# Batch normalisation, two group normalisations and two convolution stacks as one pipeline of 48 strips

## The reference

```
x = x + attention(gn(x))                        # dilated, shifted windows
x = x + relu(batch_norm(grouped_conv3x3(gn(x))))
x = x + stack(gn(x), weights 2)
x = x + stack(gn(x), weights 3)
```

## Time and profile before

| what | value |
|---|---|
| median of three runs | 2486.26 us |
| the profiled execution | 2484.12 us |
| its span, first to last instruction | 2482.3 us |
| TensorE busy | 2034.6 us, 82% |
| VectorE busy | 1684.5 us, 68% |
| ScalarE busy | 1167.8 us, 47% |
| GpSimd busy | 1079.6 us, 43% |

### The profile page before, as it was taken

The page is one execution under the profiler, slowest core; times in us unless marked ns, Lnnn a source line. Parts: engine busy times, 40 slices in busy tenths (PEclk is TensorE's granted clock), DMA queues, the critical chain, the costliest instruction groups (busy, mean ns, idle before and its releaser), DMA issues. The chain is left out here.

```text
span 2482.3 us, 75405 instructions
## 1 busy us (share of the span) xinstructions
PE 2034.6 (82%) x30446; PEld 1079.9 (44%) x30446; DVE 1684.5 (68%) x3438; ACT 1167.8 (47%) x2597; POOL 1079.6 (43%) x1227
## 2 busy tenths in 40 slices
PE   6588878887898899868994029999997499999996
PEld 5455545554555455535552003444442133333332
DVE  5588898889888988872223964666665456556553
ACT  6476666666666566632223414444442044433330
POOL 0277767776777777749502823222220131111100
PEclk8799999999999999979997559999999599999997
DMA  8300000000000000002224941444444323444444
GB/s 228 98 23 22 22 19 22 22 22 19 22 22 22 20 23 22 22 14 68 97 96 159 405 181 49 116 146 130 143 126 114 118 58 104 122 129 129 117 101 103
DMA packets 249921, 215.55 MB, mean 87 GB/s; under 512 B 132592, under 2 KB 237808, under 8 KB 247536
## 3 DMA queue, kind: packets, MB, share of 16 engines
q1 hardware_dynamic: 249584, 210.81, 28.6%
HBM read 78.29 MB, written 75.50 MB: 62 GB/s over the span
## 5 line engine op out<-in xcount | busy, mean ns | idle before, releaser
L1176 POOL TENSOR_SCALAR l_x<-l_x,l_scale,l_shift 128x384 f32<-128x384 f32 x192 | 155.6, 810 | 600.5 <-PE banks L1403 600.5
L418 POOL TENSOR_TENSOR at_prob<-at_prob,at_inv 128x512 f32<-128x512 f32 x288 | 294.1, 1042 | 116.7 <-DVE at_inv L558 111.5
L484 ACT ACTIVATE at_prob<-at_prob 128x512 f32<-128x512 f32 x288 | 181.9, 632 | 335.2 <-DVE at_prob L548 335.1
L1366 PE MATMUL banks<-l_a,l_taps 128*32 128x384 f32 x3456 | 310.9, 490 | 8.4 <-ACT l_r L1226 8.4
L1381 PE MATMUL banks<-l_above,l_taps 128*32 128x384 f32 x1728 | 307.4, 489 | 4.0 <-issue 1.8
L1381 PE MATMUL banks<-l_below,l_taps 128*32 128x384 f32 x1728 | 306.2, 489 | 0.0
L600 PE MATMUL banks<-at_xn,at_w 128*64 128x256 f32 x2336 | 287.5, 389 | 1.8 <-ACT at_xn L436 1.4
L1236 ACT ACTIVATE l_above<-l_below 96x384 f32<-96x384 f32 x144 | 75.5, 524 | 416.6 <-DVE l_below L1309 416.6
L1309 DVE SCALAR_TENSOR_TENSOR l_below<-banks,l_b,l_old 128x384 f32<-128x384 f32 x144 | 89.0, 618 | 218.7 <-PE banks L1381 188.7
L1295 DVE COPY l_old<-l_a 32x384 f32<-32x384 f32 x576 | 208.5, 362 | 26.1 <-ACT l_a L1213 14.9
L399 POOL TENSOR_TENSOR at_turn<-at_turn,at_tables 128x256 f32<-128x256 f32 x292 | 215.4, 759 | 1.7 <-ACT at_turn L455 1.7
(11 more groups left out here) (142 smaller groups left out, 3625.2 us busy)
## 6 DMA issues: line engine op xcount, KB each, us to landing
l_x<-x_mid SPq DMA_DIRECT2D x48, 768.0 KB, 4.4
l_rows<-l_r SPq DMA_DIRECT2D x768, 48.0 KB, 2.0
at_k_bd<-at_k SPq DMA_DIRECT2D x1168, 16.0 KB, 1.8
load_raw<-in_x SPq DMA_DIRECT2D x36, 512.0 KB, 5.0
y<-c_y SPq DMA_DIRECT2D x96, 192.0 KB
bn_y<-y SPq DMA_DIRECT2D x8, 2304.0 KB, 11.6
x_mid<-x_res SPq DMA_DIRECT2D x8, 2304.0 KB, 15.7
x_mid<-l_x SPq DMA_DIRECT2D x24, 768.0 KB, 3.7
```

Of the source, the lines that this page charges most:

```text
L418: nc.gpsimd.tensor_tensor(prob[i][p][:, :, :], prob[i][p][:, :, :], inv[i][p][:, :].unsqueeze(2).broadcast_to([P, HEADS, WIN]), ALU.mult). ...
L484: nc.scalar.activation(prob[j % 2][p][:, :, :], prob[j % 2][p][:, :, :], ACT.Exp).then_inc(s["exped"], 1)
L1366: last = nc.tensor.matmul(grid(acc(k)[block_rows(c), :]), e[:, dy + 1, dx, :], a[:, k % A_RING, rows_, dx:dx + SIDE], start=(dy, dx) == TA ...
```

## The change

`batch_norm_stage`, gn2, gn3 and both `stack_stage` calls go. `conv1_stage` also stores the centred image to HBM, next to `y`. One `tail_stage` does the rest:

```diff
-            conv1_stage(sh, c1_w, c1_b, y)
-            batch_norm_stage(sh, bn, y, x_mid)
+            conv1_stage(sh, c1_w, c1_b, both[:, 1, :], both[:, 0, :])
         sh.recycle()
-        group_norm_stage(sh, "gn2", TILES)
-        stack_stage(sh, "l2", w2, x_mid)
-        sh.recycle()
-        group_norm_stage(sh, "gn3", TILES)
-        stack_stage(sh, "l3", w3, x_mid, out)
+        tail_stage(sh, (w2, w3), bn, both, out)
```

In the convolution stage, on SP, for every group g:

```diff
+                sp.wait_ge(s["centred"], g + 1)
+                at = slice(g * C1_SPAN, (g + 1) * C1_SPAN)
+                sp.dma_start(x_dram[:, at], sh.x[:, at]).then_inc(s["x_stored"], 16)
```

Images 1 to 3 are 36 units more, placed into steps; steps -2 to 1 take three units each (places p = 0, 1, 2), steps 2 to 13 two each:

```diff
+        work_places = [(k, p) for k in range(-2, 2) for p in range(3)]
+        work_places += [(k, p) for k in range(2, 2 + IMG_STRIPS * (B - 2)) for p in range(2)]
+        prep_at = {(-2, 0): 0, (-2, 1): 1, (-1, 0): 2, (-1, 1): 3, (0, 0): 4}
+        norms = [((0, 0), None), ((0, 1), 2), ((0, 2), 8), ((1, 0), 12), ((0, 3), 14), ((1, 1), 18), ((1, 2), 24), ((1, 3), 30)]
```

```diff
+                    nc.gpsimd.tensor_scalar(work_x(n), work_x(n), minus_mean(FIRST_UNITS + n), None, ALU.subtract)...
+                    pool.wait_ge(s["relu_w"], n + 1)
+                    pool.wait_ge(s["uncentred_w"], n + 1)
+                    nc.gpsimd.tensor_tensor(work_x(n), work_x(n), work_y(n), ALU.add).then_inc(s["added_w"], 1)
...
+                    nc.scalar.activation(work_y(n), work_y(n), ACT.Relu, scale=y_scale[:, 0:1],
+                                         bias=y_shift[:, 0:1]).then_inc(s["relu_w"], 1)
...
+                    dve.wait_ge(s["added_w"], n + 1)
+                    for half in range(HALF_TILES):
+                        nc.vector.bn_stats(...).then_inc(s["counted_w"], 1)
```

The places in the steps. ScalarE, then VectorE, then TensorE, then SP:

```diff
                 keep_r(k - 2, 1)
+                work_relu(k, 0)
                 keep_a(at + TILE_LEAD + 1)
                 spread(k - 3, 2)
                 keep_a(at + TILE_LEAD + 2)
                 keep_r(k - 3, 2)
+                work_relu(k, 1)
                 spread(k, 0)
+                if k in norm_at:
+                    norm_root(norm_at[k])
                 keep_r(k, 0)
                 keep_r(k - 4, 3)
                 keep_a(at + TILE_LEAD + 3)
+                work_relu(k, 2)
```

```diff
                 keep_old(k, 0, (2, 3))
+                norm_e of step k-1
                 update(at)
+                norm_a
                 keep_old(k, 1, (0, 1))
+                norm_b
                 update(at + 1)
+                work_count(k, 0), prepare
                 find_delta(k - 3, 2)
                 keep_old(k, 1, (2, 3))
                 shift_below(k - 3, 2)
+                norm_c
                 update(at + 2)
+                work_count(k, 1)
                 keep_old(k, 2, (0, 1))
                 find_delta(k, 0)
                 keep_old(k, 2, (2, 3))
                 shift_below(k, 0)
                 update(at + 3)
+                work_count(k, 2), prepare, norm_d
```

```diff
                 fold(k - 2, 0)
+                if k - 1 in norm_at: norm_bias(norm_at[k - 1], at)
                 mix(at)
                 dense(k, 1)
+                if k in norm_at: norm_mean(norm_at[k], at + 1)
+                if (k, 0) in prep_at: prepare(1, prep_at[k, 0])
                 mix(at + 1)
                 fold(k - 3, 1)
+                if k in norm_at: norm_var(norm_at[k], at + 2)
                 mix(at + 2)
```

```diff
+                work_move(k, 0)
                 turn(k - 5, 3)
                 if k >= 0:
                     load(k + 2)
-                for q in (1, 0, 2):
-                    turn(k - 4, q)
+                turn(k - 4, 1)
+                turn(k - 4, 0)
+                work_move(k, 1)
+                turn(k - 4, 2)
                 store(k - 6)
+                work_move(k, 2)
```

More of the change, by code:

```diff
@@ L717, in conv1_stage @@
         s = {n: sh.sem(f"c1_{n}") for n in (
[L718 removed]
+            "w_in", "b_in", "picked", "spread", "tables", "centred", "conv", "y_kept", "counted",
+            "x_stored")}
         y_out = [sh.sem(f"c1_y_out{i}") for i in range(Y_RING)]
@@ L979, in stack_stage @@
-        zero = sb("zero", [P, SIDE])
-        s = {n: sh.sem(f"{tag}_{n}") for n in (
-            "w_in", "taps_in", "chain", "pe_chain", "grids_zeroed", "a_zeroed", "s1", "a",
-            "top", "bottom", "z", "f", "x_scaled", "updated", "counted")}
-        conv, delta, lower, upper, shifted, old_kept = (
-            [sh.sem(f"{tag}_{n}{i}") for i in range(3)] for n in (
-                "conv", "delta", "lower", "upper", "shifted", "old_kept"))
-        relu = [sh.sem(f"{tag}_relu{q}") for q in range(BLOCKS)]
@@ L1069, in stack_stage @@
+        y_t1, y_t2, y_scale, y_shift = (sb(f"y_{n}", [P, 1]) for n in ("t1", "t2", "scale", "shift"))
+        work = sb("work", [P, 2 * WORK_UNITS, HALF_STRIP])
         x = sb("x", [P, X_RING, STRIP])
@@ new lines, in tail_stage @@
+        w_in, taps_in = ([sh.sem(f"l_{n}{kind}") for kind in range(2)] for n in ("w_in", "taps_in"))
+        first_in = [sh.sem(f"l_first_in{k}") for k in range(IMG_STRIPS)]
+        y_in = [sh.sem(f"l_y_in{i}") for i in range(2 * WORK_UNITS)]
+        work_in, work_out = ([sh.sem(f"l_{n}{i}") for i in range(WORK_UNITS)] for n in ("work_in", "work_out"))
+        conv, delta, lower, upper, shifted, old_kept = (
+            [sh.sem(f"l_{n}{i}") for i in range(3)] for n in (
+                "conv", "delta", "lower", "upper", "shifted", "old_kept"))
```

612 lines of the change are left out of this document (389 added, 223 removed).

## The result

The changed kernel is slower. Over the runs taken side by side it takes 2551.43 us (median of 4, 2540.49 to 2564.0) against 2485.49 for the kernel before (median of 4): ratio 1.0267, 95% interval 1.0215 to 1.0319. The forecast of 2442 us and its range up to 2480 both miss. The profiled execution took 2564.0 us, the longest of the four, with a span of 2561.8; what follows explains its 79.5 us over the span before. The medians are 66 us apart, so some 13 of the 79.5 us belong to this execution.

The account below looks back on a forecast made before the run. TensorE was taken to bound the strip stages, DMA and VectorE batch normalisation. Terms -75.7 - 34.5 + 36 + 9 + 21.6 = -43.6 us gave 2442 us, with 2390 to 2480 holding 8 in 10.

Parts of the forecast that it names:

- part 2: Convolution stage: 24 added stores of the centred image, 768 KB each, hide beside idle DMA engines; cost 0, at most +4 us.
- Part 4: Fill up to strip 6, with images 1 to 3 in it: T(6) at 1527.6 against 1562.10, -34.5 us (-59 to -18).
- part 3: Tail's start to first ready normalisation: statistics, weight preparation, memsets, image 0's units, one normalisation; sum 54.2 plus 1, ready at 1397.7.
- Parts 5 and 6: Steps 6 to 13 with two added units each: longer chain +36 us, slower clock after the hole +9 us.
- the two links: Steps 6 to 13: ReLU behind ScalarE's keep, count before VectorE's next delta, put into the closing loop; +4.5 us a step.
- part 6: Steps 6 to 13: a 5 us TensorE hole lowers the clock, 0 to 1.9 us a step, taken as 1.1; +9 us.
- rival B: Steps -2 to 13: links cost more through slow GpSimd, VectorE waits and queued loads; +32 us, 2474; chance 0.15.
- Part 7: Normalisations inside steps 8, 12, 14, 18, 24, 30: TensorE's products wait for VectorE, 3.6 us each; +21.6 us (11 to 30).
- Part 1: Joint between the stacks: one pipeline removes a drain, a normalisation with preparation and a fill; -75.7 us.
- C: Steps 2 to 13: clock stays low, +10.4 us a step, 2558; 0.08 with a wholly different fault of its size.

Follow-up runs that it names:

- run 5: Changed kernel with ScalarE's second added ReLU before its spread and VectorE's second count behind delta 0 and its shift: 2500.98 us, ratio 1.008.
- run 1: Kernel before, plus only the 24 stores of the centred image (768 KB each) in the convolution stage, read by nobody: 2547.95 us, ratio 1.0279.
- run 10: Changed kernel with reordered added work and VectorE adding units; old y stores, x stored uncentred in 96 tiles in the attention stage: 2383.02 us, ratio 0.9613.
- run 6: Changed kernel with both edits: y stores cut by tile, and the added ReLU and count moved in the order: 2456.09 us, ratio 0.9908.
- run 9: Changed kernel with y stores by tile, reordered added work and VectorE adding units; normalisation products one place later on TensorE: 2394.66 us, ratio 0.9652.
- run 11: The edits of run 9 and run 10 together, the later normalisation products and x stored in the attention stage: 2371.15 us, ratio 0.9564 to the kernel before.
- run 4: Kernel before, with only its y stores cut by tile (outer dimension 32, not 4): 2489.03 us, ratio 1.0032.
- run 3: Changed kernel with the four y stores of each group cut by tile instead of by quarter of the channels: 2501.39 us, ratio 1.0089.

## Why the prediction was wrong

**The step that failed: part 2, "Storing the centred image in the convolution stage", which says "Cost 0".** It measured +82.4 us in the profiled run (+68.4 in that of run 5); run 1 shows +63 for the store alone, run 10 that without it nothing of the loss is left. My reasons were a share of 0.22, a landing time of 3.7 us from another stage, and an SP that mostly waits. The last was right (79.4 of 100 us). The share was misread: it is a mean over 16 engines, and over a row that begins 50 us before the first convolution product. From 1200 to 1300 it lay at 0.28 without a dip through five stretches of 20 us, in which the stores were issued in bursts of 2.8 us every 8.6. A load that comes in bursts and shows no dip is a resource that is busy between them too: four or five packets in flight nearly all the time. The 3.7 us were those of a wide store among others, and neither its issue nor what it did to the narrow ones was in it.

**Part 4, the fill: mis-sized.** -14.5 for -34.5. The ready point came 58.5 us after the start of the tail (55.2 by part 3, whose preparation term, 1457.65 to 1469.0 less 1.5, comes to 9.85 and not 9.6), strip 2 52.6 us behind it (58.3): both close. Steps 2 to 5 took 94.0 us where I took 71.6, a value between two bounds; the upper one, 21.9 a step, would have given 87.6. They are steps with the same two units, and were on average nearly as long as the steps after them, 23.5 us for 25.7 (single ones 15.2 to 28.5).

**Parts 5 and 6, the steps with added units: mechanism right, size short.** +66.3, with the two normalisations in it, for +52.2. TensorE's hole was forecast at 5 us and measured 5.02 and 5.15; the two links stood where they were put, and run 5 took them out. The clock term was 1.1 a step, and it was mis-sized. The eight dense products behind the holes lost 11.0 us by their own (28.2 for 8 x 2.15), and the products after them lost some more. It shows in the way from the first to the second dense product of a step, here in the step at 1654.64, then in the one of the kernel before at 1683.75:

```profile
1661.41 2.14 PE L1575 MATMUL banks<-l_a,l_taps 128*32 128x384 f32 x24
```

```profile
1688.92 2.15 PE L1366 MATMUL banks<-l_a,l_taps 128*32 128x384 f32 x24
```

That is 6.77 us for 5.17. In the eight steps it sums to 57.3 for 41.4; less 0.9 for two bias products in it, the half clock cost 15.0 us, 1.9 a step. By the rule that part 6 cites, of the Trainium skill, "TensorE: Matmul & The Clock Gate", section "HAM oscillation — how this bites in real kernels", the sum would have carried 15 for my 9. The trace agrees with the size, though two of eight holes, the shortest (3.87, 3.77), brought the clock down not at all or in part. What I left out are VectorE's copies beside GpSimd: "No engine is overbooked" was true, but two engines got in each other's way, 2.8 us a step in run 6. The earlier trace rows had a sign of it: VectorE's adds beside GpSimd with a maximum of 2592 ns for a median of 1009. I had priced that only for the prologue, +4, and in rival B.

**Part 7: right in the first stack, wrong at its last.** Steps 14, 18 and 24 cost 11.4 together for 10.8, 1.7 of it the half clock behind the hole that step 13 leaves. Step 30 is the one in which output transposes share the bank, and it cost 12.1 with the clock. Moving the products (run 9) gave 1.4 for each of 14, 18 and 24 and 4.3 at the last.

**Part 1 held:** strip 24 to strip 30 are 107.5 us, six steps of 17.37 and 3.3 for the one normalisation in them, where part 7 has 3.6. By these rows the merge is worth 75.7 us of the 108.6 that run 11 gains; most of what was lost around it was avoidable.

**The rivals.** B had the right kind of fault in the steps, GpSimd beside VectorE, and named a queue that moves more, but as a 32 us addition and for the steps alone. C, the only one on the slower side, did not occur: the clock came back within each step. None had the convolution stage, and so the chance of slower was 0.08.

## What to carry to other kernels

A DMA share that lies flat at a quarter while the queue issues in bursts can be, as here, a quarter of the engines that is full, and not three quarters free: look at it in short windows, and at the outer dimension of the transfers, before adding others beside them. Move such a transfer to the stage where the queue idles, not to the stage where its data happen to be ready. And price work given to GpSimd twice, once in its own time and once in what it takes from VectorE's copies: here VectorE's one fused instruction of 1.00 us was cheaper for VectorE itself than two on GpSimd.

## What the runs showed of the hardware

- A narrow store (outer dimension 4) beside a wide one: four of them took SyncE 8.4 us to issue in the changed kernel (median of the stage), 2.8 alone, and 2.2 beside it when cut to an outer dimension of 32. Alone they kept four or five packets in flight 93% of the time.
- TensorE idled more by "issue" with more wide stores in the convolution stage: 10.3 us (before) and 8.9 (run 10) with narrow stores alone, 17.1 with narrow y and wide x (run 1), 23.7 with y by tile (run 4), 36.0 with y by tile and wide x (run 3).
- A VectorE copy of 32x384 took 350 to 364 ns on average without long GpSimd work and 596 in steps with it (run 6); a bn_stats took 538 to 561 in all of them.
- TensorE's granted clock behind a hole, in steps with some 17 us of dense work: after holes of 4.70 to 5.52 us the dense product took 3.50 to 4.07 us, after 3.77 and 3.87 it took 2.83 and 2.15, after 3.60 in run 5 it took 3.20, and after up to 1.68 (run 5) always 2.15. At steps 30 and 31 waits of 0.94, 0.62 and 1.83 us close together also brought it to 0.50.
